# Batch attention's prologue re-ordered: first loads and expert choice in the stage before, 16-bit counts, row numbers between the first maxima

## What is computed

```python
xn = _layernorm(x)
Q = (xn @ Wq.T + bq).reshape(B, S, H, dk)        # B=32, S=256, H=16, dk=8; K, V alike
scores = jnp.einsum('bqhd,bkhd->hbqk', Q, K)
attn = jax.nn.softmax(scores, axis=1)            # over the batch b, for each h, q, k
heads = jnp.einsum('hbqk,bkhd->bqhd', attn, V)
logits = xn @ gate_w.T + gate_b
top1 = jnp.argmax(logits, axis=-1)               # which of 8 experts runs on the token
x = x + heads @ Wo.T + bo + ffn_of_expert(top1)(xn)
```

## Time and profile before

| | |
|---|---|
| median of 3 runs | 1594.35 us (1589.63, 1594.35, 1595.75) |
| span of the profiled execution | 1588.9 us, 0.7 under the fastest run; its own time is not listed apart |
| busy share of the span | PE 88%, VectorE (DVE) 70%, PEld 68%, GpSimd (POOL) 66%, ScalarE (ACT) 46% |
| first stage | 0 to about 100.5 us |
| prologue of attention | 100.5 to about 138 us |
| rest of the attention stage | 138 to about 790 us |
| the other stages | to 1588.9 us |

### The profile page before, as it was taken

How to read it: one execution, slowest core, us unless ns; L and a number is a source line. 1 busy time by engine, 2 the same in 40 slices (tenths; PEclk the granted TensorE clock), 3 DMA queues, 4 the chain that set the end, 5 groups by cost and what they waited for, 6 DMA issues and landing times. The chain is left out here.

```text
span 1588.9 us, 41679 instructions
## 1 busy us (share of the span) xinstructions
PE 1391.6 (88%) x14844; PEld 1079.3 (68%) x14845; DVE 1119.5 (70%) x1911; ACT 725.7 (46%) x1565; POOL 1043.7 (66%) x763
## 2 busy tenths in 40 slices
PE   6868999999999999999679995988999799999970
PEld 4635666666666666666469993776777599999960
DVE  5648999999999999999955563756754333333329
ACT  7824555555555555555334442643434244444430
POOL 6724888888888888888924444557777544444430
PEclk9969999999999999999799996999999899999995
DMA  6875233333333333331335442101111122222228
GB/s 218 281 221 149 63 86 88 88 88 88 88 88 88 88 84 84 82 86 29 122 104 181 143 126 87 41 30 44 58 41 46 39 68 66 65 67 65 66 74 288
DMA packets 112206, 155.17 MB, mean 98 GB/s; under 512 B 17856, under 2 KB 85696, under 8 KB 107200
## 3 DMA queue, kind: packets, MB, share of 16 engines
q1 hardware_dynamic: 78496, 106.64, 24.5%
q0 software_dynamic: 13344, 27.92, 5.3%
q10 hardware_dynamic: 20224, 18.65, 3.7%
HBM read 95.33 MB, written 57.82 MB: 96 GB/s over the span
## 5 line engine op out<-in xcount | busy, mean ns | idle before, releaser
L1002 POOL TENSOR_TENSOR V<-Ex,R 128x4096 f32<-128x4096 f32 x64 | 475.2, 7425 | 71.5 <-DVE R L854 71.4
L939 ACT ACTIVATE Ex<-pB 128x512 f32<-128x512 f32 x512 | 305.5, 597 | 264.1 <-PE pB L739 255.7
L832 DVE TENSOR_REDUCE mg<-pA 128x128 f32<-128x2048 f32 x128 | 288.8, 2256 | 8.4 <-PE pA L722 8.4
L848 DVE TENSOR_REDUCE Z<-Ex 128x64 f32<-128x2048 f32 x128 | 290.7, 2273 | 3.3 <-ACT Ex L939 3.1
L1087 POOL DMA_INDIRECT y_d<-x1yb,x1xb x136 | 131.8, 969 | 151.2 <-DVE x1yb L1224 144.7
L734 PE MATMUL pB<-mh,identb 128*128 128x512 bf16 x512 | 196.4, 384 | 0.2
L734 PE MATMUL pB<-ml,identb 128*128 128x512 bf16 x512 | 193.4, 378 | 0.0
L749 PE MATMUL pO<-V,Vh 128*8 128x128 f32 x4096 | 162.7, 280 | 13.5 <-POOL V L1002 13.5
L1764 POOL DMA_INDIRECT xs_d<-d_xn,d_idx x128 | 130.9, 1023 | 42.1 <-issue 35.3
L1224 DVE COPY x1yb<-x1pY 128x128 f32<-128x128 f32 x136 | 39.7, 292 | 160.8 <-PE x1pY L1121 160.7
L1110 PE MATMUL x1pU<-x1xT,x1w1s 128*128 128x128 f32 x1088 | 145.0, 276 | 0.2 <-ACT x1xT L1148 0.2
(11 more groups left out here) (265 smaller groups left out, 2530.2 us busy)
## 6 DMA issues: line engine op xcount, KB each, us to landing
w<-qs_d SPq DMA_DIRECT2D x48, 192.0 KB
w<-ks_d SPq DMA_DIRECT2D x48, 192.0 KB
qk<-qs_d SPq DMA_DIRECT2D x48, 192.0 KB
qk<-ks_d SPq DMA_DIRECT2D x48, 192.0 KB
x1xb<-xs_d SPq DMA_DIRECT2D x136, 64.5 KB, 1.8
f_ye<-y_d SPq DMA_DIRECT2D x16, 512.0 KB, 4.9
qs_d<-parts SPq DMA_DIRECT2D x16, 384.0 KB, 2.9
ks_d<-parts SPq DMA_DIRECT2D x16, 384.0 KB, 3.2
```

The lines of the kernel that those rows point to most:

```text
L832: dve.tensor_reduce(mg[:, :, g], pA[:].rearrange("p b q -> p q b"), AX.X, ALU.max).then_inc(b_red, 1)
L848: dve.tensor_reduce(Z[:, q], Ex[:, j, q, :], AX.X, ALU.add).then_inc(b_sum, 1)
L939: act.activation(Ex[:, j, :, BG * g:BG * (g + 1)], pB[:, g % 2, :, :].rearrange("p b q -> p q b"), ACT.Exp).then_inc(b_exp, 1)
L1002: pool.tensor_tensor(En[:, j % 2, :, :].rearrange("p b q -> p q b"), Ex[:, j, :, :], R[:, j % 2, :].unsqueeze(2).broadcast_to([P, P, B]), ...
```

## The change

Five edits, all ahead of or in the first units of attention:

1. SyncE requests the first half of head 0 (six requests) at the end of the first stage, once the stores of tiles 0 to 7 have landed. It no longer waits there for the last stores; that wait stands behind the barrier.
2. VectorE chooses the experts in the first stage: tiles 0 to 11 after tile 11, tiles 12 to 15 after tile 15. The marks `oh` are 16-bit and lie in `wqkv`, which is loaded later.
3. Hits are counted from 16-bit marks with 16-bit `belowb` and `onesb`, into `pO`. Two more constants are made on GpSimd at the end of the first stage.
4. Counting, row numbers and the clearing of `pO` stand between the first group maxima. The fourth `s1_group` stands in the body of unit 0, which has its own places for the groups; `keep_busy` calls are 6 (first stage), 2, 5 and 5 instead of 10 and four times 5.
5. ScalarE's nine small loads go out one a unit from unit 4; the V store stands between its first two casts; GpSimd's `low_part` 0, 1 and 2 are spread over its own start, the third behind `pad_rows`.

```diff
@@ first stage, SyncE
                 for s in range(2):
-                    sp.wait_ge(a_pd[s], 16 * NT)
-                for q in range(4):
-                    sp.wait_ge(a_xnd[q], 4 * NT)
+                    sp.wait_ge(a_pd[s], 8 * NT)
+                settle(sp, settled)
+                load_q(sp, 0, 0, 0)
+                load_k(sp, 0, 0, 0)
@@ first stage, VectorE
+                def choose_experts(t0, t1):
+                    n = slice(t0 * SUB, t1 * SUB)
+                    shape = [P, (t1 - t0) * SUB, E]
+                    dve.wait_ge(a_vs, t1)
+                    link(dve.tensor_reduce(rowm[:, n], lg0[:, n, :], AX.X, ALU.max))
...
-                sweep(NT, body, 4)
+                for t in range(NT):
+                    body(t, t % 4)
+                    if t in CHOOSE_AFTER:
+                        i = CHOOSE_AFTER.index(t)
+                        choose_experts(CHOOSE_AFTER[i - 1] + 1 if i else 0, t + 1)
@@ attention, SyncE
-                load_q(0, 0, 0)
-                load_k(0, 0, 0)
-                load_k(0, 0, 1)
-                load_q(0, 0, 1)
+                for s in range(2):
+                    sp.wait_ge(a_pd[s], 16 * NT)
+                settle(sp, settled)
+                load_k(sp, 0, 0, 1)
+                load_q(sp, 0, 0, 1)
@@ attention, TensorE, in the body of a unit
-                            if g % (NBG // NM) == 0:
+                            if u == 0:
+                                if g == 2:
+                                    s1_group(NM + 1, 0, 0, 1, 1)
+                                elif g >= 4:
+                                    s1(g // 2 - 2)
+                            elif g % (NBG // NM) == 0:
                                 s1(g // (NBG // NM))
@@ attention, ScalarE
-                            if g == 6 and (j < 2 or not is_last(h, H)):
+                            if g == (7 if u == 0 else 6) and (j < 2 or not is_last(h, H)):
                                 high_part(u + 2, (j + 2) % 4)
...
-                act.wait_ge(b_qk[0][0], LOADS)
+                high_part(0, 0)
                 store_v(act, VPART * len(V_AT))
-                act.wait_ge(b_row, 1)
-                high_part(0, 0)
                 high_part(1, 1)
```

More of the change, by code:

```diff
@@ L398, in _ @@
                 sweep(NT, body, 4)
+                keep_busy(pX[:, 0, :], 6)
             @block.scalar
@@ L760, in pv_waits @@
                             pe.wait_ge(b_vh[s], 8 * (h - s) + 16)
+                    if v == 0 and g == 0:
+                        pe.wait_ge(b_z, 1)
                     if j % 2 == 0 and g % (NBG // 2) == 0 and v >= 2:
@@ L808, in count_before @@
                       .then_inc(b_cnt, 1)
-                pe.wait_ge(b_z, 1)
-                count_before()
-                keep_busy(pA[:, 0:BG, :].rearrange("p b q -> p (b q)"), 10)
-                for j in range(2):
-                    s1_waits(0, 0, j)
-                    for g in range(NM):
-                        s1_group(NM * j + g, 0, 0, j, g)
-                        if j == 0 and g == 0:
-                            pe.wait_ge(b_row, 1)
-                        keep_busy(pB[:, 1, :, :].rearrange("p b q -> p (b q)"), 5)
+                keep_busy(warm, 2)
@@ L820, in _ @@
+                s1_waits(0, 0, 0)
+                s1_group(0, 0, 0, 0, 0)
+                count_hits()
+                keep_busy(warm, 5)
+                s1_group(1, 0, 0, 0, 1)
+                count_before()
+                keep_busy(warm, 5)
+                s1_waits(0, 0, 1)
+                s1_group(NM, 0, 0, 1, 0)
                 sweep(H, body)
@@ L977, in _ @@
                 pad_fill(pool)
+                low_part(0, 0)
                 link = chain(pool, c_m, 0)
@@ L986, in _ @@
                                         base=SPAN - 1 - P, pattern=[[-1, P]], channel_multiplier=1))
-                for u in range(3):
-                    low_part(u, u)
                 pad_tags(pool)
+                low_part(1, 1)
                 pad_rows(pool)
+                low_part(2, 2)
                 def body(h, s):
```

168 lines of the change are left out of this document (98 added, 70 removed).

## The result

| | before | changed |
|---|---|---|
| median, 10 runs each | 1592.85 us (1589.63 to 1595.75) | 1597.24 us (1595.28 to 1600.55) |
| ratio to the kernel before | | 1.0034, 95% interval 1.0021 to 1.0047 |
| the same change measured again, 12 runs (35 of before) | 1591.44 | 1597.51; 1.0036, 1.0021 to 1.0052 |
| span of the profiled execution | 1588.9 us | 1595.1 us |

One disturbed execution of the changed kernel, of 1825.63 us, is left out of the ratio and of the bounds shown; its median is 1597.24 us with it and 1596.84 without. By the ratio the change costs 0.34%, 5.4 us; the two medians are 4.4 us apart. The forecast was 1.7 us gained. 1597.24 lies in its range (1586 to 1600), and under the 0.5% that were to count as a change; but the interval holds neither the forecast nor no change, and the sign is the other one.

The account below looks back on a forecast made before the run. VectorE was taken as the bound to the end of attention; first maximum 7.1 us earlier, path from there to unit 3's first maximum 5.4 longer, so 1.7 gained: 1594.35 - 1.7 = 1592.6 us, range 1586 to 1600.

Parts of the forecast that it names:

- The choice costs 2.0 us in the first stage: First stage, behind tile 11: VectorE's choice takes 2.9 us with 0.91 spare, so the stage's tail shifts 2.0 us.
- Rival A: Prologue: choice vanishes in tile 14's 5.69 us wait, loads land earliest, clock up; gain 6.3, 1588.1 us; chance 0.17.
- The order of six loads: End of first stage, SyncE: three q, three k requests follow its last store at 99.8; barrier at about 103.9.
- First maximum: Start of attention, VectorE: starts at 109.6 instead of 116.66, 7.1 us early, first group slow at 2.1 us.
- Row numbers: Between third and fourth maximum on VectorE: 3.65 us replace a wait of 1.16, costing 2.5 us.
- ScalarE's order: Unit 1's cast ahead of the first exponential holds it until 126.3; fifth maximum 129.4 instead of 126.7, 2.7 us.
- At nothing: Claimed free: ScalarE's nine loads, GpSimd's indirect stores, second half of head 0, 16-bit counting, V store.
- The second half of head 0: Before the third group: issued from 103.9, lands 6.75 to 10 us later, needed at 116.1, so costs nothing.
- I take 7.5: First half of head 0, q and k bursts: landing takes 7.5 us, between 6.75 and 8.7, giving 107.35.
- From there to the anchor: First maximum to unit 3's first maximum, behind which VectorE never waits: path 5.4 us longer, ending at 136.3.
- rival C: First groups: clock stays at 1.2 GHz to unit 0, rising after about 116 us; 6.7 us slower, 1599.4; chance 0.15.
- D: SyncE's first loads: late first byte has another cause than ScalarE's loads, bytes 3.1 us later, 1595.7; chance 0.13.

Follow-up runs that it names:

- choice13: Changed kernel with the first part of the expert choice behind tile 13 instead of tile 11; ratio to the kernel before 1.0003, repeated 1.0007.
- small_at_once: Changed kernel with eight of ScalarE's nine small loads at once behind the barrier again; ratio to the kernel before 1.0043.
- before_spread: Kernel before with only ScalarE's nine small loads going out one a unit from unit 4; ratio to the kernel before 1.0005.
- warm12: Changed kernel with twelve `keep_busy` matmuls instead of two ahead of the first group; ratio to the kernel before 1.0020.
- all3: Changed kernel with unit 1's cast behind the fourth exponential, choice behind tile 13, and twelve `keep_busy` ahead of the first group; ratio to the kernel before 0.9999.
- rows_first: Changed kernel with the row numbers ahead of the first maximum, `pO` cleared beneath the wait for the second group; ratio to the kernel before 1.0031.
- no_early: Changed kernel with the first loads back behind the barrier and SyncE's waits as before; ratio to the kernel before 1.0062.
- cast_late: Changed kernel with ScalarE's cast of unit 1 moved from ahead of the first exponential to behind the fourth; ratio to the kernel before 1.0011.
- cast_choice13: Changed kernel with unit 1's cast behind the fourth exponential and the choice behind tile 13; ratio to the kernel before 0.9999.
- rows_first_third: Third profile of rows_first, same kernel, on another chip; one execution, no ratio; first maximum of unit 3 at 136.5 us.
- fill_gap: all3 with twelve `keep_busy` beneath the row numbers in the free half of `pB`, and GpSimd's third `low_part` ahead of `pad_rows`; ratio to the kernel before 0.9973.
- rows_first_all: rows_first with cast behind the fourth exponential, choice behind tile 13, third `low_part` ahead of `pad_rows`; ratio to the kernel before 0.9952, 1584.76 us.
- before_layout: Kernel before with only the changed kernel's buffers reserved, for the addresses, no instruction added or moved; ratio to the kernel before 0.9999.

## Why the prediction was wrong

**Right.** *The choice costs 2.0 us in the first stage:* tile 11 to 15 takes 23.0 us on the mean of nine profiles against 21.0, and choice13 takes it away. Rival A's cheap end for it is refuted: in the trace, tile 14's wait ended 18.84 us behind tile 11's `rem` instead of 16.44. That it ended at 87.8 and not at 90 was chance, since tile 11 itself came 2.5 us sooner in that execution; "at 88 would mean A", as I had put it, was a bad test, because it named a time of the clock on the wall and not a distance. *The order of six loads:* the first request stands 5.25 us behind tile 15's `rem`, forecast 5.14. *First maximum:* 109.28, forecast 109.6, but by luck, as the next paragraph says. *Row numbers:* third to fourth maximum 5.95, forecast 5.94. *ScalarE's order:* the exponential right behind the second cast, at 127.93, forecast 126.3. *At nothing:* small loads and V store; small_at_once and before_spread bear it out for the loads. GpSimd's margin was there too: its third `low_part` is done 7.6 us ahead of unit 2 on TensorE in the change, and at least 4.4 us ahead in every other kernel's trace. *The second half of head 0* cost nothing in the change, but by luck: I had it land 6.75 to 10 us behind its request. In warm12, all3 and rows_first, where the third group waits for it, it is 12.6 to 14.0 us; only the slow rows ahead of that group hide this in the change.

**Wrong, first: "I take 7.5" for the landing.** From request to landing it is 9.6 us, 2.1 more. The upper end I had given was 8.7, from bursts that had DMA to themselves; here tile 15's stores, the fill of the spare rows and the requests for the second half were under way as well. Which of them costs is not shown: in no_early the last store had landed (100.3) before the first request (100.86), and it took 11.6 us; over all sixteen traces of the change and its variants it is 9.5 to 11.6. The first maximum came at the forecast time all the same, because the whole execution was ahead: tile 11 by 2.5 us. Behind tile 15's `rem` it came at 16.8, forecast 14.9.

**Wrong, second, and the step that turns the sign: "From there to the anchor".** 30.25 us instead of 26.7. By its terms: second maximum 5.00 behind the first (forecast 4.25), third 4.69 (3.45), fourth 5.95 (5.94), fifth 7.71 (6.15), the last two 3.45 each, as forecast. All three that are over stand beside TensorE rows at 1.2 GHz. I had the clock half up at the second group and up from the third, and gave rival C 0.15; C came true in part: the clock rose at 118.4, past the 116 us that I had named as its sign, the second group took 1.91 us, the third 1.47, and the fifth fell into the second low stretch. It cost 3.55 of the 6.7 us that I had given it. And its mechanism was incomplete. I saw too little warming ahead of the groups; I did not see that TensorE idles behind the fourth group, and that the clock falls *again*. Two waits make that stretch, and each alone goes with a low clock: the row numbers (3.55 us idle in cast_late, cast_choice13 and all3, where no exponential is held and the clock falls at 128.1, 126.3 and 122.9), and the held exponential (3.71 us in rows_first_third, where the row numbers are out of the gap and it falls at 122.3). In the change they lie one upon the other, 6.20 us. So the stall taken from the front came back twice, as the wait for ScalarE and as slow groups behind it. In fill_gap, where the gap is filled and the exponential isn't held, and in rows_first_all, where both waits are gone, the fifth maximum follows at 3.45 us and the clock stays up.

Together: 0.1 to the request, 2.1 for the landing, 0.3 less from the landing to the first maximum (1.9 instead of 2.25), 3.55 behind it, 5.4 us. The anchor is 47.0 behind tile 15's `rem`; the forecast, 136.3 against 94.66, had put 41.6. The forecast's gain of 1.7 less 5.4 is a loss of 3.7 on the path; measured are 5.4 and 5.7. That 1597.24 still lies in the range says little for the forecast, which was a gain: the range reached up to 1600 to take in rivals C and D and the noise.

**The reading of the baseline.** I took one profiled execution for the kernel. From tile 15 on it was a fair one (45.4 against a mean of 45.05), but its tile 11 came at 71.5 where the other three have 68.8 to 69.2, so its anchor was the latest of four, and its way behind the anchor the shortest (1448.0 of 1448.0 to 1453.9). That did not bend the forecast, which goes by differences, but it hid the cost of the choice in the first comparison. Also, the profiled executions' own times, where listed, are 1.7 to 1.8 us above their spans, so the "5.5 above the span" that I added was mostly the distance of that execution from the median.

**Sum of the change by its parts:** 1.8 us for the choice in these two profiles, 2.3 us more from tile 15 to the anchor (47.35 against a mean of 45.05), 1.1 us less because tile 11 came sooner in those executions: 3.0 us at the anchor. Measured: 5.4 and 5.7. Of the other 2.5 us the traces show 1.8 behind the anchor on the mean, within their scatter.

**Open:** whether the change really costs 1 to 2 us behind the anchor. before_layout makes the addresses an unlikely reason, and before_spread (1450.9 behind the anchor) the later small loads. Open is also why choice13's median gained 5 us on the change with the anchor no earlier, so whether the choice behind tile 11 costs 2 us, as the traces have it, or more, and why rows_first's median is 4 us above its three profiled executions.

## What to carry to other kernels

A prologue is worth what it does to the instruction behind which the bounding engine never waits again; bringing the first result forward is worth only what every link up to there lets through, and the links to check first are in-order neighbours that wait for something later than what is queued behind them (here a cast ahead of the exponentials). Put work of the bounding engine into a wait that it has anyway, ahead of its first result, and not between results where it idles its suppliers: idle time on TensorE can cost once more in clock. Before a fraction of a per cent is explained from traces, profile the kernel before more than once, and compare distances from a common mark, not times.

## What was unexpected of the hardware

- The granted clock fell from 2.4 to 1.2 GHz within an idle stretch of 6.2 us of TensorE (the change), and within or up to 1.5 us behind one of 3.55 us (cast_late, cast_choice13, all3). It stayed there 6.8 to 20.4 us in the kernels with the held exponential. Twelve matmuls ahead of the first group did not prevent it (warm12), while twelve in the gap did (fill_gap, one trace).
- Six loads of 192 KB, three q and three k, which I had put at 6.75 to 8.7 us from bursts in a quiet queue, took 9.5 to 11.6 us here, and the six behind them 12.6 to 14.0 where a group waits for them.
- With nine small loads on ScalarE's queue, SyncE's queue stayed without a byte for 4.5 us behind its first request, though the DMA engines were busy for a share of only 0.18 in the last microsecond of it; with the loads gone its first byte moved 1.6 us behind the request.
- Executions of one and the same kernel differ by 12 us (1585.64 to 1597.39 in 35), and go with the mean granted clock (correlation -0.86).
